# Who computes the means of x1: one VectorE subtraction per pair of tiles, or two one-column ScalarE operations out of PSUM

## The reference, cut to what matters

```python
h = _layernorm(x) * (1 + ca) + sa
x = x + ga * attention(h)                      # x1
h = _layernorm(x) * (1 + cb) + sb              # needs the mean and the variance of each row of x1
gate_probs = softmax(h @ Wg + bg)
_, top_idx = top_k(gate_probs, 2)
x = x + gb * moe(h, gate_probs, top_idx)
```

## Time and profile before

| | |
|---|---|
| median of three runs | 787.0 us (786.61 to 788.0) |
| the profiled execution | 786.93 us, of it the span from first to last instruction 785.2 us |
| TensorE busy | 735.9 us, 94% of the span |
| VectorE busy | 560.9 us, 71% |
| ScalarE busy | 470.5 us, 60% |
| GpSimd busy | 365.1 us, 46% |
| granted TensorE clock | 0.977 of full speed on average |

### The profile page before, as it was taken

How to read it: one execution, slowest core, us unless ns; L and a number is a source line. 1 busy time by engine, 2 the same in 40 slices (tenths; PEclk the granted TensorE clock), 3 DMA queues, 4 the chain that set the end, 5 groups by cost and what they waited for, 6 DMA issues and landing times.

```text
span 785.2 us, 16562 instructions
## 1 busy us (share of the span) xinstructions
PE 735.9 (94%) x5716; PEld 672.5 (86%) x5716; DVE 560.9 (71%) x1253; ACT 470.5 (60%) x912; POOL 365.1 (46%) x326
## 2 busy tenths in 40 slices
PE   5899999999999999934999999999999999999994
PEld 4778888888888887712999999999999999999994
DVE  6899888777777633888667667675776776776653
ACT  5565665565645536595667556656665765765543
POOL 2642433424422119201364655556655555656554
PEclk9999999999999999957899999999999999999998
DMA  7500000000000135861262632526344244233323
GB/s 283 182 1 1 1 2 2 2 1 1 1 2 1 55 108 192 262 132 35 75 164 41 171 57 60 148 57 162 57 123 94 42 125 92 41 51 60 48 56 48
DMA packets 45602, 59.57 MB, mean 76 GB/s; under 512 B 8002, under 2 KB 38788, under 8 KB 45412
## 3 DMA queue, kind: packets, MB, share of 16 engines
q0 software_dynamic: 14352, 21.85, 15.4%
q1 hardware_dynamic: 31188, 36.93, 14.8%
HBM read 40.49 MB, written 18.27 MB: 75 GB/s over the span
## 4 chain that ended last, share of the span: by engine, by line
PE 87%; DVE 8%; ACT 1%; POOL 1%; issue 1%; DMA 1%; POOLq 0%; DVEq 0%; SPq 0%; ACTq 0%
PE ps L1847 24%; PE ps L1861 24%; PE ps L1625 11%; PE ps L1582 10%; PE ps L1650 4%; PE ps L1634 3%; PE ps L1730 3%; PE ps L1821 2%; DVE at_hi L1360 2%; PE ps L1704 1%; PE ps L1564 1%; DVE ln_s L1040 1%; DVE q_exp L1077 1%; DVE q_max L1076 1%; DMA x_all<-in_L_attn_x 1%
## 5 line engine op out<-in xcount | busy, mean ns | idle before, releaser
L989 ACT ACTIVATE hid<-ps,b_col 128x256 f32<-128x256 f32 (+1 forms) x232 | 105.8, 507 | 113.4 <-PE ps L1847 109.0
L1861 PE MATMUL ps<-w_hi,hid_hi 128*128 128x256 f32 x544 | 154.1, 283 | 0.0
L1861 PE MATMUL ps<-w_hi,hid_lo 128*128 128x256 f32 x544 | 151.7, 279 | 0.0
L1861 PE MATMUL ps<-w_lo,hid_hi 128*128 128x256 f32 x544 | 151.7, 279 | 0.0
L1499 DVE TENSOR_TENSOR hid_lo<-hid,hid_hi 128x512 fp32r<-128x512 f32 (+1 forms) x116 | 91.0, 784 | 73.0 <-ACT hid_hi L993 72.9
L1847 PE MATMUL ps<-xT_hi,w_hi 128*128 128x256 f32 (+1 forms) x464 | 139.4, 300 | 1.6 <-DVE xT_lo L1451 1.6
L1847 PE MATMUL ps<-xT_lo,w_hi 128*128 128x256 f32 (+1 forms) x464 | 139.2, 300 | 0.0
L1847 PE MATMUL ps<-xT_hi,w_lo 128*128 128x256 f32 (+1 forms) x464 | 139.0, 299 | 0.0
L702 POOL DMA_INDIRECT out<-y,y_id x68 | 117.0, 1721 | 40.4 <-issue 16.1
L584 POOL TENSOR_TENSOR q_n<-q_exp,q_rec 128x1024 f32<-128x1024 f32 (+1 forms) x33 | 61.0, 1852 | 147.6 <-DVE q_rec L1084 147.6
L687 POOL DMA_INDIRECT listed<-xrows,gid x86 | 94.4, 1097 | 42.2 <-POOL gid L683 23.8
(11 more groups left out here) (246 smaller groups left out, 1417.2 us busy)
## 6 DMA issues: line engine op xcount, KB each, us to landing
w_raw<-in_L_ffn_W SPq DMA_DIRECT2D x16, 1024.0 KB
x_all<-in_L_attn_x SPq DMA_DIRECT2D x8, 512.0 KB, 10.2
out<-x_all SPq DMA_DIRECT2D x8, 512.0 KB, 3.0
xrows<-x_all SPq DMA_DIRECT2D x8, 512.0 KB, 5.0
listed<-xrows,gid POOLq DMA_INDIRECT x86
out<-y,y_id POOLq DMA_INDIRECT x68
wqk_raw<-in_L_attn_w_qkv SPq DMA_DIRECT2D x2, 512.0 KB, 6.2
wqk_raw<-in_L_attn_w_qkv SPq DMA_DIRECT2D x1, 1024.0 KB, 10.5
```

Source lines behind the costliest of these rows:

```text
L989: ins = act.activation(hid[:, m, 0:T], src, ACT.Gelu_apprx_tanh, bias=b1_col[:, e, m:m + 1])
L1861: last = pe.matmul(ps[:, bank, 0:D], a, w_, start=m == 0 and st, stop=m == M - 1 and sp_)
```

## The change

ScalarE computes `low` for the pairs 2 to 15, one tile at a time: `low = -1.0 * ps + low_mean` on one column, with `low_mean` as the bias. VectorE's L1278 is gone. `gate_part(q)` waits for `s_x1` of the pair in place of `s_mean`; `square(q)` waits for both new operations of its own engine. The gate part of the last pair moves from behind the loop to in front of its squares.

```diff
             def gate_part(q):
-                act.wait_ge(s_mean, q - LATE + 1)
+                act.wait_ge(s_x1, 2 * q + 2)
                 b = AT + 2 * (q % AHEAD)
+                act.wait_ge(s_mean0, 1)
+                for i in range(2):
+                    t = 2 * q + i
+                    act.activation(low[:, t:t + 1], ps[:, b + i, D + E:D + E + 1], ACT.Identity, scale=-1.0, bias=low_mean[:, t:t + 1]).then_inc(s_mean, 1)
                 act.activation(raw_lg[:, 2 * q:2 * q + 2, :], ps[:, b:b + 2, D:D + GW + E], ACT.Copy).then_inc(s_lg, 1)
...
             def square(q):
...
-                    act.wait_ge(s_mean, q - LATE + 1)
+                    act.wait_ge(s_mean, 2 * (q - LATE + 1))
...
-                if q < PAIRS - 1:
-                    gate_part(q)
+                gate_part(q)
                 square(q)
...
-            gate_part(PAIRS - 1)
             lo_hot(1)
...
             def residual(q):
...
-                if q >= LATE:
-                    dve.tensor_tensor(low[:, 2 * q:2 * q + 2], low_mean[:, 2 * q:2 * q + 2], ps[:, b:b + 2, D + E], ALU.subtract).then_inc(s_mean, 1)
```

## The result

The changed kernel takes 790.2 us (median of six runs, 789.15 to 791.22) against 787.43 us before (six runs, 786.61 to 788.54): ratio 1.0029, 95% interval 1.0018 to 1.0040, that is 1.4 to 3.1 us slower. Forecast were 789.7 us and a sum of 2.8 us. The profiled execution took 790.32 us.

The account below looks back on a forecast made before the run. One serial line through TensorE, VectorE and ScalarE was taken to bound the kernel, ScalarE pacing TensorE at pairs 2 to 5. 1.48 + 0.15 + 0.30 + 0.38 + 0.46 = 2.8 us on 786.93 gave 789.7 us, range 787.9 to 791.2.

Parts of the forecast that it names:

- step 2: VectorE's `root(0)` comes 2.28 us late, delaying pair 9's copy and so `attend(12)` by 0.26 us; half counted, 0.15.
- The new operation: ScalarE's one-column Identity out of PSUM with bias from memory: 0.26 us, taking 0.17 us of the queue.
- Step 1: Pairs 2 to 5: ScalarE's later gate copies delay TensorE at `attend(8)` by 3 x 0.38 + 0.34 = 1.48 us.
- Steps 3, 4 and 5: ScalarE's pairs 13, 14 and 15 on the serial line: 0.30, 0.38 and 0.46 us, the last including its gate copy.
- Sum at `root(1)`: All five steps together delay `root(1)` by 2.77 us, rounded to 2.8.
- From `root(1)` on all shifts together: Behind `root(1)` everything moves by the same 2.8 us; the experts start at 376.4 for 373.66.
- Rival B: TensorE's clock returns at another moment after its restart: only 1.3 us slower, 788.2; chance 0.10 on the cheap side.
- A: The bias costs nothing extra, or the small pieces hide in ScalarE's queue: 1.4 us, 788.3; chance 0.13.
- C: VectorE's first root becomes the bound: 3.3 to 4 us, 790.2 to 791; chance 0.23 together with B's dear side.
- D: Identity not in resident tables, two table loads of 1.28 us per pair: 15 us, 802 with the rest; chance 0.01.

Follow-up runs that it names:

- six operations a pair: The whole change plus four more ScalarE operations of the same kind per pair, into a tile nothing reads: 794.76 us, ratio 1.0086 to before.
- before with the gate part first: The kernel before, means by VectorE, each gate part moved in front of its pair's weight conversion: 788.07 us, ratio 0.9995.
- the version with VectorE's means and three moves: Kernel before with gate parts ahead of weight conversions, last gate part ahead of its squares, `lo_hot(0)` behind the last pair's squares: 786.90 us, ratio 0.9983.

## Why the prediction was right

The time, the sign and the mechanism up to `root(1)` were right, apart from one term (step 2); what was said of the time behind `root(1)` was not. The steps, each against the distances:

- *The new operation.* 0.26 us forecast, 0.244 measured; in the queue 0.145 apart (0.17). By the Trainium skill ("ScalarE: Activation LUTs", section "What ACT_TABLE_LOAD costs") it would have been 0.28; for the bias operand alone the page has about 93 ns, and the two kernels differ by 91. The pair costs 0.41 us (0.38). The square starts 0.46 us behind the first new operation, exactly where its wait for its own engine was put; the 0.02 more lie between the square and the instruction behind it (0.42 for 0.40 us).
- *Step 1, 1.48:* 1.50, and the kernel with the pairs 2 to 5 alone has the same 1.50. Two terms in it were off and cancel: a pair costs 0.41 in place of 0.38, the copy is held up by 0.28 in place of 0.34.
- *Step 2, 0.15:* **nothing**, the one mis-sized term. `root(0)` came 2.41 us later (2.28 forecast), but `residual(9)` only 1.23 later: the root lasted 0.83 us less, most of it by L1284 (0.17 in place of 0.87), and the sum followed at once, without the 0.27 us gap of the earlier trace rows. The copy of pair 9 ended at 321.48, 0.97 before `attend(12)`. The prediction had seen that 0.87 could shrink and counted half. The mechanism exists: with six operations a pair it binds.
- *Steps 3, 4 and 5, 0.30, 0.38 and 0.46:* 0.33, 0.40 and 0.49, read off the first squares of the pairs 13, 14 and 15 (1.83 - 1.50, 2.23 - 1.83, 2.72 - 2.23); the pairs 13 to 15 alone make 1.24.
- *Sum at `root(1)`, 2.77:* 2.74. That it fits to 0.03 is partly luck: the 0.15 that isn't there is made up by some 0.10 that the other steps measured above their forecast. *"From `root(1)` on all shifts together":* **wrong by 0.42.** The move of the last gate part takes GpSimd's sums from beside the root. I had followed the copy only to the wait that it releases ("gets it earlier than it needs") and not to what the released work disturbs. The 0.37 us of shorter root operations is shown in both directions, 0.27 of it with the move alone and 0.37 with the move undone; the other 0.05 is within the 0.12 us by which the traces scatter between `ranks(1)` and the restart.
- *Rival B, the clock.* The clock's return moved by itself: 3.4 us after the restart before, 5.2 in the whole change (0.8 us in the first 48 products), and 5.0, after a restart at 375.06, in the kernel with the pairs 6 to 12 alone, whose distances are those of before:

```profile
379.00:380.00 1.00, 1.00 (x4) 0.50 0.42 102
380.00:381.00 1.00, 1.00 (x7) 0.95 0.09 34
```

It varies from 3.3 to 6.0 us over the thirteen traces, with no relation to the edit that I can see, and the first 48 products take 10.07 to 11.35 us with it. The start of stage B, ahead of every edit, varies more, from 302.18 to 303.87. These two and the 1 us by which the rest of stage C varies set how far a single execution can be trusted; of the executions without a trace none of this was seen. The profiled execution is 3.4 us longer (788.6 - 785.2), with 2.3 us at the experts' start, for: 0.4 ahead of stage B, 2.3 in it, 0.8 by the clock, less 0.1 behind. What the change does is the 2.3 us. The medians give 2.8, in whose interval 2.3 lies; that the difference is the clock was not shown. So it is luck that the medians differ by 2.77 us, the very sum of the prediction: what the trace bears out is 2.74 at `root(1)`, of which 0.42 came back.
- *Rivals A, C and D.* A is priced: without the bias operand 1.46 us at `root(1)` (1.4 forecast). C doesn't bind at two operations a pair and does at six; where between was not tried. D: the trace has the same two table loads as before, at the start and at 363.13, and none among the pairs. (The chances that the prediction lists add up to 1.01.)

## What to carry to other kernels

Ask of an added operation where on the serial line it stands, not how long it takes: of fourteen pairs seven cost nothing, four cost 1.5 us and three 1.2. Look at the weight loads for the stalls that a busy TensorE hides, and at the queue of the engine that releases them: the remedy was to put the 34-column copy for which TensorE waits in front of the 1.05 us of work for which nobody does. And follow an edit past the wait it releases: work that starts earlier or later on one engine can slow the work of another beside it.

## What the runs showed of the hardware

A one-column ACTIVATE out of PSUM takes 153 ns, with a bias from memory 244, and neighbours of the latter start 145 ns apart. VectorE instructions of 16 columns that take 0.17 to 0.19 us alone take 0.31 to 0.42 when they begin while one of GpSimd's sums is under way, and end 0.03 to 0.05 us after it; eight of 256 columns take 2.77 to 2.93 us beside the three sums in place of 2.13. The first instruction of `root(0)` took 0.85 to 0.88 us in five traces in which it started beside GpSimd's last weight part (before, pairs 13 to 15, before with the gate part first, before with the last gate part moved, and the version with VectorE's means and three moves); in all five it ended 0.02 to 0.03 us after GpSimd's first sum (before: 314.62 + 0.87 = 315.49, and 315.47). In the other eight traces, where it started later, it took 0.17 or 0.18. That GpSimd is the cause here too was not tried by itself. After its restart TensorE ran at 1.2 GHz for 3.3 to 6 us until the granted clock was back at 2.4.
